# Attention with block sums: where the blocks of P are added up for the softmax denominator

## The reference

```python
x = x + _layernorm(attn(_layernorm(x)))      # x: 4 x 2048 x 512, 16 heads of 32
x = x + _layernorm(ffn(_layernorm(x)))       # one of 8 matrices, chosen by argmax
...
att = einsum('bhtd,bhsd->bhts', q, k) * (1.0 / sqrt(D))
att = where(mask == 0, -inf, att)            # mask: s <= t and s % 4 != 3
att = softmax(att, axis=-1)
y = einsum('bhts,bhsd->bhtd', att, v)
```

## Time and profile before

| | |
|---|---|
| time, median of 3 runs | 2567.81 us (2565.41 to 2570.93) |
| the profiled execution | 2565.07 us |
| its span, first to last instruction | 2563.3 us |
| granted TensorE clock, mean | 0.986 of full |
| PE busy | 2410.8 us, 94% |
| DVE busy | 1804.7 us, 70% |
| ACT busy | 1494.5 us, 58% |
| POOL busy | 1427.6 us, 56% |

### The profile page before, as it was taken

The page is one execution under the profiler, slowest core; times in us unless marked ns, Lnnn a source line. Parts: engine busy times, 40 slices in busy tenths (PEclk is TensorE's granted clock), DMA queues, the critical chain, the costliest instruction groups (busy, mean ns, idle before and its releaser), DMA issues.

```text
span 2563.3 us, 43166 instructions
## 1 busy us (share of the span) xinstructions
PE 2410.8 (94%) x15380; PEld 924.9 (36%) x15380; DVE 1804.7 (70%) x4820; ACT 1494.5 (58%) x2654; POOL 1427.6 (56%) x1318
## 2 busy tenths in 40 slices
PE   4899999998999999999999999999999999999986
PEld 2343333333343333333344343333234433333322
DVE  7767777777477777767567767767738766777764
ACT  5545566556655556557655565665665555565663
POOL 2235465665656365576754637557756454656623
PEclk9899999999999999999999999999999999999998
DMA  6223030111233231021122313002204131301001
GB/s 189 56 43 95 22 86 23 36 48 41 46 88 73 55 73 49 7 53 41 43 65 66 99 36 89 14 18 55 51 23 99 41 97 42 77 12 32 28 1 33
DMA packets 224352, 137.46 MB, mean 54 GB/s; under 512 B 146730, under 2 KB 196618, under 8 KB 224138
## 3 DMA queue, kind: packets, MB, share of 16 engines
q1 hardware_dynamic: 222310, 134.65, 20.8%
q10 hardware_dynamic: 1828, 0.07, 0.0%
HBM read 39.69 MB, written 16.78 MB: 22 GB/s over the span
## 4 chain that ended last, share of the span: by engine, by line
PE 59%; DVE 20%; POOL 7%; issue 6%; ACT 4%; DMA 2%; SPq 1%; ACTq 0%; POOLq 0%; DVEq 0%
PE psO L1198 12%; PE acc L1160 10%; PE acc L1180 9%; PE psU L1215 8%; PE acc L1131 6%; PE acc L1133 6%; PE acc L1132 6%; DVE MP L939 4%; POOL P L717 3%; ACT P L841 3%; DVE acc L935 3%; DVE STA L907 3%; DVE XR L918 2%; PE acc L1184 1%; DVE XB L918 1%
## 5 line engine op out<-in xcount | busy, mean ns | idle before, releaser
L841 ACT ACTIVATE P<-acc,EX 128x512 f32<-128x512 f32 (+2 forms) x1920 | 1076.6, 636 | 476.4 <-PE acc L1180 237.1
L939 DVE TENSOR_REDUCE MP<-acc 128x1 f32<-128x512 f32 (+1 forms) x1088 | 719.4, 679 | 220.3 <-PE acc L1160 217.1
L717 POOL TENSOR_TENSOR P<-P 128x512 f32<-128x512 f32 x546 | 683.7, 1281 | 151.0 <-ACT P L841 150.5
L1160 PE MATMUL acc<-KST,QST 96*128 96x512 f16 (+10 forms) x2112 | 584.0, 335 | 40.5 <-DVE MP L935 22.2
L935 DVE CUSTOM_DVE_ANT_0 acc<-acc,CB 128x96 f32<-128x96 f32 (+7 forms) x1024 | 450.3, 454 | 241.0 <-PE acc L1160 239.4
L1180 PE MATMUL acc<-QST,KST 98*128 98x512 f16 (+2 forms) x1920 | 571.7, 356 | 23.8 <-DVE MP L935 9.3
L1198 PE MATMUL psO<-P,V 128*32 128x512 f32 (+2 forms) x3840 | 464.8, 556 | 11.7 <-ACT P L841 9.3
L1160 PEld LDWEIGHTS acc<-KST,QST 96*128 96x128 f16 x2112 | 192.4, 97 | 393.1 <-issue 108.0
L722 POOL TENSOR_TENSOR SC<-SC 128x512 f32<-128x512 f32 x64 | 82.3, 1286 | 449.7 <-DVE SC L973 449.6
L1180 PEld LDWEIGHTS acc<-QST,KST 98*128 98x128 f16 x1920 | 179.3, 97 | 375.5 <-issue 154.5
L1215 PE MATMUL psU<-P,ONES 128*32 128x512 f32 (+2 forms) x2688 | 300.4, 519 | 0.0
(11 more groups left out here) (140 smaller groups left out, 2832.7 us busy)
## 6 DMA issues: line engine op xcount, KB each, us to landing
QST<-QKH SPq DMA_DIRECT2D x128, 128.0 KB, 3.2
XR<-in_L_attn_x_dram SPq DMA_DIRECT2D x60, 256.0 KB, 3.0
out_dram<-XR SPq DMA_DIRECT2D x60, 256.0 KB, 2.1
KST<-QKH SPq DMA_DIRECT2D x128, 96.0 KB, 2.7
XB<-in_L_attn_x_dram SPq DMA_DIRECT2D x48, 252.0 KB
QST<-QKL SPq DMA_DIRECT2D x64, 128.0 KB, 3.3
KST<-QKL SPq DMA_DIRECT2D x64, 96.0 KB, 2.7
XB<-in_L_attn_x_dram SPq DMA_DIRECT2D x20, 256.0 KB, 3.5
```

The lines of the kernel that those rows point to most:

```text
L717: e.tensor_tensor(P[:, acc, a, :], P[:, acc, a, :], P[:, buf, a, :], ALU.add).then_inc(g_s, 1)
L841: e.activation(P[:, p_buf[u, g, sb_], a, t0:512], bank(*step)[:, t0:512], ACT.Exp, scale=EX[:, 1:2]).then_inc(a_e, 1)
L939: e.tensor_reduce(maxima(u, g)[:, r, a, ci:ci + 1], bank(*s)[:, 0:n], AX.X, ALU.max).then_inc(v_m, 1)
L1160: i = e.matmul(bank(*s)[:, 0:n], QST[0:96, h, 128 * r:128 * r + 128], KST[0:96, h, c0:c0 + n], start=True, stop=True)
```

## The change

The sums of whole blocks leave PE. With j > 0, `added(j)` is now every block from 1 to 3j, so that 3, 6, 9 blocks are added at j = 1, 2, 3, and three sums are left per group: the accumulator and the two narrow blocks. At j = 0 nothing changes: blocks 0, 1 and 2 have a sum each. `ADDS` gives the adds of heads 2 and 3 to DVE in every unit with j > 0; in the last unit DVE has all four heads of group 3 as well. The costs and the table LONG in the plan stay as they are. Line numbers in the changed kernel are 3 lower.

```diff
--- before.py
+++ after.py
@@ -1,10 +1,6 @@
 import concourse.bass as bass
 from concourse import mybir
 from contextlib import ExitStack
-
-
-def on_pe(j, sb):
-    return sb >= 3 * j or sb % 3 == 1
 
 
 def chunks(w):
@@ -23,12 +19,12 @@
 
 def added(j):
 
-    return [s for s in range(1, 3 * j) if not on_pe(j, s)]
+    return list(range(1, 3 * j + 1)) if j else []
 
 
 def sum_blocks(j):
 
-    return [s for s in range(j > 0, 3 * j + 1) if on_pe(j, s)] + (["acc"] if j else []) + [3 * j + 1, 3 * j + 2]
+    return (["acc"] if j else [0]) + [3 * j + 1, 3 * j + 2]
 
 
 def p_blocks(NB, NJ):
@@ -61,6 +57,7 @@
 
     LONG = ((15, 20, 26, 27), (40, 40, 31, 35), (51, 51, 41, 42), (63, 57, 46, 58))
     AHEAD, QK, ROW, V, FINISH, EACH = 45, 25, 30, 25, 12, 6
+    ADDS = ((), (2, 3), (2, 3), (2, 3))
     LAG = {"pe": 150, "act": 250, "dve": 220, "gp": 200, "sp": 2600, "hbm": 0}
     BANKS = 6
     MOST = {"psX": 2, "psW": 2, "psM": 3, "psS": 4}
@@ -258,7 +255,7 @@
 
     def adder(self, u, g, a):
 
-        return "dve" if u == self.NU - 1 and (g == 3 or g == 2 and a > 1) else "gp"
+        return "dve" if a in self.ADDS[u % self.NJ] or u == self.NU - 1 and (g == 3 or g == 2 and a > 1) else "gp"
 
     def last_use(self, u, g, sb, a):
```

## The result

| | before | after |
|---|---|---|
| time, median | 2566.61 us (2561.59 to 2570.93, 4 runs) | 2765.46 us (2764.24 to 2771.52, 4 runs) |
| ratio, 95% interval | | 1.0777 (1.0756 to 1.0797) |
| span | 2563.3 us | 2763.7 us |
| granted TensorE clock | 0.986 | 0.958 |
| PE idle in the span | 152 us | 367 us |

What follows compares the result with a forecast made beforehand. PE was taken to set the time, with 2 to 6% idle. 2565.07 - 54.5 (units) + 24 (new wait) = 2534.6 us for the profiled execution; the runs' median is 2.7 higher, so 2537 us, range 2475 to 2630.

Steps and rivals of the forecast that it cites:

- What leaves TensorE: Sums of whole blocks at j = 1, 2, 3: 144 sets leave PE at 0.89 us each, 128 us in all.
- The price of a VectorE add: Each add arriving on DVE was taken at 0.80 us, between a floor of 0.60 and an upper value of 0.93.
- The share that VectorE can hold: Highest DVE busy share of a whole unit, allowed at 0.96; it set the forecast at j = 2, 3 and the last unit.
- the sum's own lines: Unit forecasts with DVE as bound: j = 2 (128.6 + 38.4)/0.96 = 174 us, j = 3 (144.5 + 57.6)/0.96 = 210.5 us.
- The new wait: PE's matmul on the accumulated block waits for adds of block 3j: 0.5 us for each of 48 groups, +24 us.
- The rival on the slower side: VectorE bounds the units at share 0.95, adds meet POOL at random and cost 0.93 us: 2619 us, chance 0.39.
- The full gain: Rival: VectorE keeps up at 0.60 us an add, units go by PE over 0.95: 2465 us, chance 0.14.
- The signs: Expected in the profile: PE busy down 120 to 150 us, adds over 0.8 us; j = 3 losing more than j = 2 would be wrong.

Runs made afterwards that it cites:

- e2: Changed kernel with each of the 594 VectorE adds replaced by a memset of 128 x 1, so these adds are left out; 2435.9 us.
- e11: Changed kernel with only the order changed: the plan is told 1150 ns per VectorE add and 1500 ns per POOL add; 2775.1 us.
- e1: Changed kernel with each of the 594 VectorE adds replaced by a one-operand maximum over the same block; 2480.6 us.
- e8: Changed kernel with POOL's 558 adds replaced by memsets of 128 x 1, VectorE's 594 adds kept; 2467.0 us.
- f1: Kernel before, sums on PE as before, but all adds on VectorE alone, two heads in one instruction; 2586.2 us.
- e5: Changed kernel with all adds on POOL except those VectorE had in the last unit before; the sums stay away from PE; 2817.1 us.
- e3: Changed kernel with the two VectorE adds of a block made as one double instruction, 297 in place of 594; 2683.3 us.
- e9: Changed kernel with two one-operand maxima in a row in place of each VectorE add; 2776.3 us.

## Why the prediction was wrong

- **What leaves TensorE: right.** 0.89 us for each of 144 sets, 128 us. e2 shows 122. (The lower price read from rows 4 is 1.86 - 1.00 = 0.86, not 0.87, which changes nothing.)
- **The price of a VectorE add: the step that failed.** I took 0.80 us, "between the ends", under an upper value of 0.93. It is 1.15. The mechanism was named and right: both engines shut each other out, and the one in flight finishes first. But the size came from adds at a random moment beside a POOL that is busy 60 to 68%. Here a POOL instruction that is held up stays in flight longer, so that 75% of the adds start beside one, with 0.80 us of it still to go (counted over the trace); 0.75 x 0.80 = 0.60 us of waiting, where 0.20 was assumed. An add directly behind another waited 0.78 us on average. The 30 adds of before said little: 20 of them belong to a group in which POOL adds nothing. The one of 1.17 us was the typical case, near the middle of the 594. Too little was counted by 594 x (1.15 - 0.80) = 208 us of VectorE time. With 1.15 in place of 0.80 and nothing else changed, the prediction's sum gives 2708 us: 171 of the 228 us by which it missed.
- **The share that VectorE can hold: too high.** I allowed 0.96 where the fullest 40 us showed 0.91. The units hold 0.88 to 0.93, and no run here has a unit over 0.94. With 1.15 us and 0.91 the sum's own lines give (128.6 + 55.2)/0.91 = 202 us at j = 2 and (144.5 + 82.8)/0.91 = 250 at j = 3, against 195 and 242 measured, with VectorE busy for 180 and 219 us and not 184 and 227. At j = 1 the forecast had PE as the bound and 3.5 us of gain; VectorE was at 0.88 there and 7 us were lost.
- **The new wait: in its bounds.** 43 us against 24, between 0 and 61. 32 of the 43 fall in the four units with j = 1, the ones where VectorE was least full. Taking most of it away did not help: e11 has 10 us of it and is no faster.
- **The rival on the slower side** had the mechanism and the sign. Its price of 0.93 us and its 0.95 made 2619 out of it. Its upper bound should have been the whole POOL add behind each DVE add, 0.60 + 1.28 = 1.88 us, since the single case seen did wait for the rest of one; with that end in the range the slower side should have had the larger chance.
- **The full gain** would have needed adds that nothing holds up: e1, 2481 us, is about what it would have been. Its -10 us for the last unit does not follow from its own rule, which gives (183.8 - 14.2)/0.95 = 178.5 us, 19.5 less; e1 had 6 less.
- **The signs.** PE's busy time was to fall by 120 to 150 us whatever the total did, and fell by 14, mostly because the clock was left out (see the last section). That j = 3 lost more than j = 2, 21.8 against 19.4 us, was one of the signs of being wrong.

The Trainium skill ("SBUF — State Buffer", section "Who interferes with whom") states that a VectorE instruction with two SBUF inputs contends with a GpSimd instruction that reads SBUF, and that a `tensor_reduce` never does. Both hold here: the adds with two SBUF inputs were held up (1.18 us), and the maxima of e1, which are `tensor_reduce` with one input, were not (0.68 us).

## What to carry to other kernels

Price an operation that moves to an engine at what it costs beside the work that stays where it was. If two engines exclude each other, take one whole instruction of the other as the upper end, not the mean over random moments: that end was 1.88 us here, and the slowest of 594 took 1.80.

The receiver's share of a stretch alone does not tell whether the move pays. At j = 2, VectorE at 91% went with units of 171 and 169 us in e1 and e8, faster than the 175 of before, but 86% went with 182 us in f1, where PE had kept its sums. No unit held over 0.94, so a forecast should not fill an engine further than that.

An idle share of an engine is not room either. POOL had 33 to 53% of a unit free. Giving it all adds (e5) gained 4 us at j = 1 and lost 18 and 52 at j = 2 and 3, where the exponentials wait for buffers that its four adds in a row hold.

## What the runs showed of the hardware

- The turn goes back and forth. In the pair shown, a POOL add that has been held up gets in ahead of the next DVE add, which started after it and then waits for its end: 2.35 us for two adds that need 1.2.
- A DVE add that was held ends 0.54 to 0.60 us after the POOL instruction that held it, for 411 of 594; a double one ends 1.08 to 1.10 us after it, for 214 of the 297 in e3.
- The granted clock fell as PE's idle time grew, from 0.986 to 0.958, and to 0.962 in e9, where the maxima were not held up. Two stretches of the changed kernel in a row, columns as in rows 2, the granted clock third from the end:

```profile
1240.00:1256.00 16.00, 15.11 (x95) 5.32 (x87) 12.09 (x29) 10.50 (x20) 7.43 (x7) 1.00 0.17 47
1256.00:1270.00 14.00, 10.56 (x51) 2.33 (x48) 14.00 (x21) 7.70 (x12) 14.00 (x10) 0.88 0.28 69
```

In the first PE is busy 15.1 of 16 us at 1.00, in the second 10.6 of 14 at 0.88: part of the time, the lower level of 1.2 GHz. An estimate from the means over the span: with two levels, one half of the other, 0.958 is 2764 x 0.042 x 2 = 232 us at the lower level, against 72 us before. The 160 us more at half the clock make about 80 us more of busy time, and this is most of the reason why PE's busy time fell by only 14 us: in e1, with the same work on PE and a clock of 0.985, it is 2306.5 us, 91 less. How much of the 199 us the lower clock costs, beside the waits that brought it on, no run here separates.
